# Every step of the mixing tables is issued one unit later in the experts' stage

## The reference, cut to what matters

```python
def _L0_attn_ref(x, time_decay, time_first, key_w, value_w, recep_w, out_w):
    v = x @ value_w.T
    r = sigmoid(x @ recep_w.T)
    # per channel, with the state (aa, bb, pp) from (0, 0, -10000), at each time:
    #   ww = time_first + pp;   p = max(pp, ww)
    #   wkv = (e^(pp-p) aa + e^(ww-p) v) / (e^(pp-p) bb + e^(ww-p) + 1e-6)
    #   ww2 = time_decay + pp;  p2 = max(pp, ww2)
    #   aa = e^(pp-p2) aa + e^(ww2-p2) v
    #   bb = e^(pp-p2) bb + e^(ww2-p2);   pp = p2
    return (r * wkv) @ out_w.T

def _L0_ffn_ref(x, ...):                  # 8 experts, the best 2 for each token
    gate_dense = ...                      # softmax scores of the two chosen experts
    expert = (silu(x @ w1e.T + b1e) * (x @ w3e.T + b3e)) @ w2e.T + b2e
    y = einsum('etd,te->td', outs, gate_dense)
    z = (silu(x @ ws1.T + bs1) * (x @ ws3.T + bs3)) @ ws2.T + bs2
    return y + z

xn = layernorm(x)                         # x: 2 x 2048 tokens of 256 channels
x = x + _L0_attn_ref(xn, ...) + _L0_ffn_ref(xn, ...)
```

## Time and profile before

| | |
|---|---|
| median of three runs | 465.22 us (464.21, 465.22, 469.5) |
| the profiled execution | 466.4 us |
| its span in the trace | 464.7 us, mean granted clock 0.981 |
| `route` | from 0 to about 68 us |
| `run_experts` | from about 68 to 260 us |
| `mix` | from about 260 us to the end |

### The profile page before, as it was taken

The page is one execution under the profiler, slowest core; times in us unless marked ns, Lnnn a source line. Parts: engine busy times, 40 slices in busy tenths (PEclk is TensorE's granted clock), DMA queues, the critical chain, the costliest instruction groups (busy, mean ns, idle before and its releaser), DMA issues.

```text
span 464.7 us, 8281 instructions
## 1 busy us (share of the span) xinstructions
PE 444.1 (96%) x2535; PEld 370.9 (80%) x2535; DVE 366.3 (79%) x680; ACT 240.9 (52%) x396; POOL 236.0 (51%) x224
## 2 busy tenths in 40 slices
PE   4898989979999999999999899999999999999997
PEld 4453657858888888888888778888898989898987
DVE  5968969878787887878766589996878778797963
ACT  4686835678668595967665633332423241333231
POOL 4234787544858666489846287743251607062000
PEclk9799879999999999999999999999999999999999
DMA  8999942356664865433473792635334453624011
GB/s 252 396 351 277 270 104 79 92 187 209 241 222 142 268 185 170 137 128 105 139 183 128 255 330 82 200 140 166 111 122 158 123 172 90 203 57 127 2 47 45
DMA packets 46145, 77.75 MB, mean 167 GB/s; under 512 B 5940, under 2 KB 32284, under 8 KB 46108
## 3 DMA queue, kind: packets, MB, share of 16 engines
q1 hardware_dynamic: 37196, 56.35, 34.9%
q0 software_dynamic: 8240, 20.88, 17.5%
q10 hardware_dynamic: 672, 0.04, 0.1%
HBM read 49.04 MB, written 28.21 MB: 166 GB/s over the span
## 4 chain that ended last, share of the span: by engine, by line
PE 44%; POOL 18%; issue 15%; DVE 9%; ACT 5%; DMA 5%; SPq 3%; POOLq 0%; DVEq 0%; ACTq 0%
POOL xg L1022 8%; PE ps_w L1571 5%; PE ps_w L1573 5%; PE ps_w L1572 5%; PE ps_w L1638 4%; PE ps_w L1640 4%; PE ps_w L1639 4%; PE ps_g L1099 4%; DMA w_lo<-w_all 3%; POOL den L1034 2%; PE ps_y L1099 2%; POOL den L1033 2%; SPq L436 2%; POOL col L1041 2%; POOL firsts L1041 2%
## 5 line engine op out<-in xcount | busy, mean ns | idle before, releaser
L1022 POOL DMA_INDIRECT xg<-xn_rows,tile_tok x71 | 72.8, 1026 | 20.2 <-issue 18.9
L1547 POOL DMA_INDIRECT yg<-expert_rows,rows x64 | 67.4, 1053 | 23.5 <-issue 17.1
L1099 PE MATMUL ps_g<-w_hi,x_hi 128*128 x142 | 56.2, 396 | 0.4 <-DVE x_lo L1268 0.4
L1099 PE MATMUL ps_g<-w_lo,x_hi 128*128 x142 | 56.3, 396 | 0.0
L1099 PE MATMUL ps_g<-w_hi,x_lo 128*128 x142 | 56.0, 395 | 0.0
L1682 ACT ACTIVATE sact<-ps_w,vec_b 128x512 f32<-128x512 f32 x32 | 22.0, 689 | 59.3 <-PE ps_w L1573 59.3
L1571 PE MATMUL ps_w<-col_hi,s_hi 128*128 128x512 f32 x128 | 50.7, 396 | 0.6 <-DVE shid L1796 0.4
L1573 PE MATMUL ps_w<-col_hi,s_lo 128*128 128x512 f32 x128 | 50.2, 392 | 0.0
L1572 PE MATMUL ps_w<-col_lo,s_hi 128*128 128x512 f32 x128 | 50.2, 392 | 0.0
L1099 PE MATMUL ps_y<-w_hi,h_hi 128*128 x142 | 43.1, 304 | 1.3 <-DVE h_lo L1284 1.3
L1277 DVE TENSOR_TENSOR hid<-ps_g,act 128x512 f32<-128x512 f32 (+1 forms) x36 | 23.7, 658 | 24.2 <-ACT act L1181 23.6
(11 more groups left out here) (256 smaller groups left out, 1273.0 us busy)
## 6 DMA issues: line engine op xcount, KB each, us to landing
expert_rows<-y SPq DMA_DIRECT2D x35, 256.0 KB, 2.2
w_lo<-w_all SPq DMA_DIRECT2D x16, 384.0 KB, 9.3
table<-mix_tables SPq DMA_DIRECT2D x8, 768.0 KB, 6.5
xT<-x SPq DMA_DIRECT2D x16, 256.0 KB, 5.6
xn_rows<-xn SPq DMA_DIRECT2D x16, 256.0 KB, 8.3
xn_columns<-xT SPq DMA_DIRECT2D x8, 512.0 KB, 3.6
col<-xn_columns SPq DMA_DIRECT2D x8, 512.0 KB, 5.4
res<-x SPq DMA_DIRECT2D x16, 256.0 KB, 3.0
```

The source lines that it names most:

```text
L1022: pool.indirect_dma_start(out=xg[b][:, t, :], out_offset=None, in_=xn_d[:, :], in_offset=bass.IndirectOffsetOnAxis(ap=tile_tok[:, first_ti ...
L1099: mm = nc.tensor.matmul(out, x[:, k, :], w[:, ds(e, 1), k, cols].rearrange("p o n -> p (o n)"), start=(k == 0 and n == 0), stop=(last and ...
L1547: pool.indirect_dma_start(out=yg[a.buf(2)][:, k, q, :], out_offset=None, in_=y_d[:, :], in_offset=bass.IndirectOffsetOnAxis(ap=picked[a.bu ...
```

## The change

A constant `LATER = 1` shifts the units in which the steps of the tables are issued, on SyncE, GpSimd, ScalarE and VectorE. What each step computes and waits for is as before. The gathers, the experts' own steps and all steps with fixed units (13, 15, 18, 22, 24, and the two splits of units 32 and 34) stay where they were. The loads into the tables' buffers move with the tables, and so does the split of the value weights' low part on GpSimd, from unit 33 to 34.

```diff
--- before.py
+++ after.py
@@ -965,6 +965,7 @@
         assert TILES == 2 * DUOS - 1
 
         LAST_V = NPIECE - 1
+        LATER = 1
 
         def sync(sp):
             def store(a):
@@ -988,8 +989,8 @@
             for a in range(DUOS + 1):
                 if a > 0:
                     store(a - 1)
-                v, r = divmod(a, 4)
-                if r == 2 and v < NPIECE:
+                v, r = divmod(a - LATER, 4)
+                if r == 2 and 0 <= v < NPIECE:
                     store_decay(v)
                 if r == (2 if v == NPIECE else 3) and 0 < v <= NPIECE:
                     store_coef(v - 1)
@@ -1003,10 +1004,10 @@
                     sp.wait_ge(c_zero, 1)
                     for q in range(Q):
                         sp.dma_start(rows[TERMS * q:TERMS * q + 3 * E + 2, q, :], b_all).then_inc(c_rows, 16)
-                if a == 4 * LAST_V + 1:
+                if a == 4 * LAST_V + 1 + LATER:
                     sp.wait_ge(t_sides, NPIECE)
                     sp.dma_start(raw_vr[:], wvr).then_inc(c_vr, 16)
-                if a == 4 * LAST_V + 4:
+                if a == 4 * LAST_V + 4 + LATER:
                     assert (LAST_V - 1) % 2 == 0
                     sp.wait_ge(coef_stored, LAST_V * 16)
                     sp.dma_start(col0[:].rearrange("p k n -> p (k n)"), columns).then_inc(c_col, 16)
@@ -1075,7 +1076,7 @@
                     cut(0, vr)
                 if r == (1 if v == NPIECE else 2) and 0 < v <= NPIECE:
                     factors(v - 1)
-                if r == 3 and v < NPIECE:
+                if r == 3 and 0 <= v < NPIECE:
                     denominator(v)
 
         def tensor(pe):
@@ -1230,14 +1231,14 @@
                 split_hi(act, i)
             cut_x(2)
             for a in range(DUOS):
-                v, r = divmod(a, 4)
+                v, r = divmod(a - LATER, 4)
                 silu(a + 1)
                 cut_h(a)
                 cut_x(a + 3)
                 if a == 0:
                     for m in range(KC):
                         receptance(m)
-                if a == 2:
+                if a == 2 + LATER:
                     halves(0)
                     exps(0)
                 if r == 1 and 0 < v < NPIECE:
@@ -1369,13 +1370,13 @@
                 if a < 2:
                     for i in range(12 + 2 * a, 14 + 2 * a):
                         split_lo(dve, i)
-                if a == 1:
+                if a == 1 + LATER:
                     grown(0)
                     differences(0)
-                if a == 2:
+                if a == 2 + LATER:
                     dve.wait_ge(t_dif, 1)
                     grown(1)
-                if a == 3:
+                if a == 3 + LATER:
                     scan_b(0)
                 if r == 0 and 0 < v <= NPIECE:
                     invert(v - 1, 0)
@@ -1392,7 +1393,7 @@
                         scan_b(v)
                     if 0 < v < NPIECE:
                         invert(v - 1, 3)
-                if r == 3 and v < LAST_V:
+                if r == 3 and 0 <= v < LAST_V:
                     differences(v + 1)
                 if a == A_ZERO + 2:
                     low_mask()
```

## The result

The changed kernel took 474.07 us (median of four runs, 472.3 to 475.74), the kernel before beside it 467.04 us (four runs, 464.21 to 469.5). The ratio is 1.0175, 95% interval 1.0135 to 1.0214: slower by 1.4 to 2.1%. That is about 8 us by the ratio and 7.03 by the two medians, where 7.9 were forecast. The forecast time was 473.1 us; that 474.07 came so near to it is partly luck, since the kernel before measured 1.82 us more than the 465.22 from which the forecast started.

The account below looks back on a forecast made before the run. TensorE, busy 96% of the span, was taken to bound the kernel. Terms -1.4 + 0.6 + 6.95 - 1.03 + 2.7 + 0.1 = +7.9 us on 465.2 gave 473.1 us, range 466 to 478.

Parts of the forecast that it names:

- The start: At unit 4's wait, moved to unit 5: 0.35 us lost where 1.75 was, -1.4 us.
- The second wait: Unit 5's 1.87 us loss, moved to unit 6: expected to stay, as `scan_b(0)` and `differences(1)` still share a unit.
- The mask: VectorE's bias-row mask in unit 15 waits for GpSimd's `factors(2)`, delaying unit 17: +0.6 us, bounds 0 to 1.6.
- upper branch: Mask case where the late differences also meet the denominators and lose a further 1 us: 1.6 us.
- the restart: Extra 0.19 us by which the unit after a TensorE wait comes late, with no idle time noted.
- lower branch: Mask case taken in the sum: it waits for the factors, without the further loss beside denominators, +0.6 us.
- `low_rows`: In unit 24, ahead of `denominator(5)`: 9.28 us delay, 2.52 slack, 6.76 reach `turn_h(27)`, +6.95 with restart.
- Unit 30: The 1.03 us lost there before goes, because GpSimd catches up in the next two units: -1.03 us.
- The clock: Behind the wait at unit 27, TensorE's clock falls to 0.50 for 5.4 us, half lost: +2.7 us.
- the clock stays: Rival: no slow clock behind the wait at unit 27, so +5.2, 470.4 us; chance 0.17.
- The end: `invert(7, 2)` and `(7, 3)` move from unit 33 to 34, ahead of `col_lo`: +0.1 us.
- GpSimd's last factors hold up `col_lo`: Rival at the end: `factors(7)` goes first and `col_lo` waits 2.4 us, giving 475.4 us; chance 0.15.

Follow-up runs that it names:

- the earlier differences: Kernel before with `differences(1)` in unit 2 behind `grown(1)`, instead of unit 3 behind `scan_b(0)`; 466.06 us, timed once.
- its doses: Changed kernel with only the first, or first two, of `low_rows`' three operations in unit 24, the rest in 26; 468.34 and 474.66 us, timed once each.
- drain in 23: Changed kernel with ScalarE's drain of the bias rows in unit 23 instead of 22; 473.11 us, timed once.
- mask in 16: Changed kernel with the mask of the bias rows in unit 16, behind the differences as in the kernel before; 475.22 us, timed once.
- two operations in 24: Changed kernel with the first two of `low_rows`' operations in unit 24 and the third in unit 26; 474.66 us, timed once.

## Why the prediction was right, point by point

- *The start.* Forecast -1.4 us, the first wait shrinking to 0.35. It shrank to 0.28, -1.47, and the steps came as forecast: behind the later start of 1.89 us, `silu(5)` was due at 100.4 and came at 100.33. The second wait stayed as forecast (1.89 for 1.87), and the earlier differences showed its cause.
- *The mask.* Forecast +0.6 us with 1.6 as the upper bound. It was 1.80, above that bound. The chain was right and its upper branch happened: the wait for the factors lasted 2.19 us, cost 0.42 at unit 17, and the differences, pushed beside the denominators, cost 1.19 at unit 18, with 0.19 for the restart behind them. The step that failed is the choice of the lower branch. The start had shown what differences beside denominators cost (3.9 us), and the sum should have taken that.
- *`low_rows`.* Forecast 6.76 us at unit 27, measured 6.47, because the slack is 2.7 rather than 2.52 and the delay 9.2 rather than 9.28. The restart of 0.19, counted here, is the 0.20 that stays at unit 28 with the clock at 1.00. The order in the queue is shown by moving `low_rows` alone, the slack by its doses, and the drain's part by moving the drain.
- *Unit 30.* The 1.03 us went, as forecast. That GpSimd catches up in the units behind, the reason given, was not tested by itself.
- *The clock.* Forecast +2.7, measured 1.48 at unit 28, or 1.68 with the restart; in three other runs 1.62, 2.31 and 2.48 with it. The mechanism was right, and this is the term that was sized too high. The prediction took all 5.4 us of the routing's row as work behind the wait. In the routing the clock had fallen at about 9.9 already, 6.8 us before it rose at 16.7. Here it was low for 6.8 us too, but 3.2 of them passed in idleness and 3.6 were work. Its rival, that the clock stays, fell. The fall in the routing of the kernel before (columns as above):

```profile
9.00:10.00 1.00, 1.00 (x8) 0.76 (x8) 0.85 (x5) 0.40 (x2) 0.00 (x0) 0.93 1.06 369
10.00:11.00 1.00, 0.01 (x1) 0.00 (x0) 0.63 (x7) 0.95 (x2) 0.00 (x0) 0.50 1.09 380
```

- *The end.* Forecast +0.1 us, with a rival in which GpSimd's last factors hold up `col_lo` by 2.4. `col_lo` took 1.17 us, no longer than before, so the rival fell. From `turn_h(35)` to the first matmul of `mix` it is 4.88 us in both kernels. VectorE was first by only 0.16 us, and it was GpSimd that lost, with 3.24 us for factors that take 2.4; in all nine profiles with later tables `col_lo` starts 0.16 or 0.17 us ahead. VectorE's and GpSimd's lines in the changed kernel:

```profile
265.90 1.17 DVE L1366 TENSOR_TENSOR col_lo<-col,col_hi 128x1024 fp32r<-128x1024 f32 x1
266.06 3.24 POOL L1042 TENSOR_TENSOR firsts<-firsts,den 128x1024 f32<-128x1024 f32 x1 [3.75 <-DVE den L1327]
```

- *The sum.* +7.9 forecast, +7.44 in the stage: the mask 1.2 too low, the clock and the restart together with `low_rows` 1.5 too high. That the two misses nearly cancel is luck, and the sum is closer than its terms are.

## What to carry to other kernels

When a group of steps is shifted in hand-written queues, look first at what is not shifted with it: the distances inside the group stay, and the cost comes from fixed steps that now stand ahead of one of the group's links in the same queue. A queue's idle time lies at certain places only, so the same 8 us of work cost 1 to 2 us right behind a link, about 7 right ahead of it with the slow clock that followed (8.15 less the drain's 0.94), and nothing in three pieces where the queue waits anyway. A cost that a trace already shows for two steps meeting (here the differences beside the denominators) belongs into the sum wherever a shift makes them meet again.

## What the runs showed of the hardware

The clock's share was not fixed, and it did not follow the idle time. These are the four runs in which the clock fell in this wait, times in us (the clock's fall and rise are read from stretches of 1 us):

| kernel | idle time | idle before the clock fell | low, from fall to rise | of it work | lost at unit 28 |
|---|---|---|---|---|---|
| changed | 6.31 | 3.1 | 6.8 | 3.6 | 1.68 |
| drain in 23 | 5.37 | 2.0 | 6.8 | 3.5 | 1.62 |
| mask in 16 | 6.31 | 4.9 | 6.8 | 5.4 | 2.48 |
| two operations in 24 | 3.87 | 2.0 | 6.8 | 5.0 | 2.31 |

The low level lasted equally long in all four, and what was lost, the restart of 0.20 included, is 0.46 to 0.47 of the work that fell into it. So the same idle time of 6.31 us cost 1.68 in one run and 2.48 in another, and one of 3.87 cost 2.31. An idle time of 1.06 us left the clock at 1.00 and cost only the restart. Low stretches elsewhere in these traces have other lengths (10.2 us in the changed kernel's routing, from 51.3 to 61.5), and what sets the moment of the fall is not shown.

One operation of VectorE on a single column took 2.19 us beside GpSimd's factors, while the mask's operation just ahead of it, with one tensor as input, took 0.14 beside the same factors. The Trainium skill, "SBUF — State Buffer", section "Who interferes with whom", says that a VectorE instruction with two SBUF inputs contends with a GpSimd instruction that reads SBUF, and that one with a single input outside the two-port modes does not. The rows agree on the first. They agree on the second if the mask's operation ran outside those modes, which no row shows.
